# Where the second layer's low weight halves are computed on the GpSimd engine of a fused mixer and two-layer attention kernel

## What is computed

```python
h = shift_token(x)                      # half of the channels from the token before
q, k, v = split(h @ wqkv[l])            # 128 x 1536
q, k = rotary_xpos(l2norm(q) * qs, l2norm(k) * ks)
x = x + local_attention(q, k, v) @ wo[l]     # 8 heads of 64, windows of 64
h = layernorm(shift_token(x))
a, g = split(h @ w1[l] + b1[l])         # 128 x 682
x = x + (a * gelu(g)) @ w2[l] + b2[l]
```

## Time and profile before

| | us |
|---|---|
| median of 3 runs | 471.41 (470.22 to 472.78) |
| the profiled execution, its own time | 471.67 |
| its span in the trace | 469.9 |
| PE busy | 359.3 |
| DVE busy | 329.7 |
| POOL busy | 298.2 |
| ACT busy | 285.0 |
| mean granted TensorE clock | 0.916 of full speed |

### The profile page before, as it was taken

The page is one execution under the profiler, slowest core; times in us unless marked ns, Lnnn a source line. Parts: engine busy times, 40 slices in busy tenths (PEclk is TensorE's granted clock), DMA queues, the critical chain, the costliest instruction groups (busy, mean ns, idle before and its releaser), DMA issues.

```text
span 469.9 us, 11254 instructions
## 1 busy us (share of the span) xinstructions
PE 359.3 (76%) x3832; PEld 295.0 (63%) x3832; DVE 329.7 (70%) x744; ACT 285.0 (61%) x852; POOL 298.2 (63%) x248
## 2 busy tenths in 40 slices
PE   2573057898788998899899989998949896768362
PEld 1352036777676877687778767876838775656342
DVE  6879864678668768867877796768767866743423
ACT  3453075777676777777867867767827773664020
POOL 2200348999999499949975994899477958520212
PEclk9996575999999999999999999999979999797857
DMA  8500230511431052115113320431015201200100
GB/s 274 174 0 0 53 110 19 125 30 30 108 79 31 1 146 61 28 29 152 30 30 105 79 58 1 130 79 31 12 38 130 55 1 28 64 12 1 23 22 22
DMA packets 42399, 28.21 MB, mean 60 GB/s; under 512 B 21700, under 2 KB 36598, under 8 KB 42358
## 3 DMA queue, kind: packets, MB, share of 16 engines
q1 hardware_dynamic: 42357, 27.68, 22.7%
HBM read 13.51 MB, written 3.15 MB: 35 GB/s over the span
## 4 chain that ended last, share of the span: by engine, by line
PE 38%; DVE 22%; POOL 17%; issue 10%; ACT 7%; DMA 3%; SPq 2%; DVEq 1%; POOLq 0%; ACTq 0%
POOL rn L483 6%; PE bank L717 5%; DVE h L1083 4%; PE bank L682 4%; PE bank L554 4%; DVE rot_sin L1059 4%; PE bank L550 4%; PE upper L666 3%; PE bank L551 3%; DVE rot_cos L1059 3%; POOL rot L519 3%; ACT probs L833 2%; POOL rot L504 2%; PE bank L610 2%; POOL rot L505 2%
## 5 line engine op out<-in xcount | busy, mean ns | idle before, releaser
L833 ACT ACTIVATE probs<-upper,neg_max 128x128 f32<-128x128 f32 x256 | 90.4, 369 | 62.6 <-DVE neg_max L1105 62.6
L483 POOL TENSOR_TENSOR rn<-floored,minus_half 128x16 f32<-128x16 f32 x32 | 93.8, 2930 | 2.7
L504 POOL TENSOR_TENSOR rot<-rot_cos,rot_sin 128x512 f32<-128x512 f32 x32 | 40.9, 1278 | 64.9 <-DVE rot_sin L1059 47.1
L1105 DVE TENSOR_REDUCE neg_max<-upper 128x4 f32<-128x512 f32 x64 | 43.1, 683 | 34.4 <-PE upper L666 34.4
L519 POOL TENSOR_TENSOR rot<-rot,rn 128x1024 f32<-128x1024 f32 x32 | 60.9, 1903 | 1.9
L550 PE MATMUL bank<-wqkv_hi,act_t_hi 128*128 128x512 f32 x96 | 44.2, 460 | 21.4 <-DVE o_tok L1117 13.3
L833 ACT ACTIVATION_READ_ACCUMULATOR probs<-upper,neg_max 128x1 f32 x256 | 52.9, 207 | 0.0
L1059 DVE TENSOR_TENSOR rot_cos<-bank,tab 128x512 f32<-128x512 f32 x64 | 43.6, 682 | 2.7 <-PE bank L554 2.2
L1059 DVE TENSOR_TENSOR rot_sin<-bank,tab 128x512 f32<-128x512 f32 x64 | 43.5, 680 | 0.0
L1066 DVE TENSOR_REDUCE ss<-sq 128x16 f32<-128x1024 f32 x32 | 38.8, 1212 | 5.2 <-ACT sq L854 5.1
L550 PEld LDWEIGHTS bank<-wqkv_hi,act_t_hi 128*128 128x128 f32 x96 | 19.0, 198 | 36.0 <-issue 23.3
(11 more groups left out here) (129 smaller groups left out, 883.1 us busy)
## 6 DMA issues: line engine op xcount, KB each, us to landing
v_mid<-v_tok SPq DMA_DIRECT2D x64, 128.0 KB, 2.3
tab_raw<-tables SPq DMA_DIRECT2D x8, 512.0 KB, 3.3
h_tok<-group_in SPq DMA_DIRECT2D x14, 128.0 KB, 3.4
x_res<-group_in SPq DMA_DIRECT2D x28, 64.0 KB, 1.8
wqkv_raw<-wqkv SPq DMA_DIRECT2D x2, 768.0 KB, 6.7
x_in<-x SPq DMA_DIRECT2D x4, 256.0 KB, 3.4
head_scale<-head_scales SPq DMA_DIRECT2D x8, 128.0 KB, 3.9
group_in<-normed SPq DMA_DIRECT2D x4, 256.0 KB
```

The lines of the kernel that those rows point to most:

```text
L483: pool.tensor_tensor(rn[:, 0:2 * HEADS], floored[:, 0:2 * HEADS], minus_half[:, :], ALU.pow).then_inc(rn_ready, 1)
L504: pool.tensor_tensor(rot[cur.par][:, :, 0:32], rot_cos[:, :, 0:32], rot_sin[:, :, 32:64], ALU.add).then_inc(rot_added, 1)
L833: last = act.activation(probs[:, h, :], s_bank[half][:, (h % 4) * P:(h % 4 + 1) * P], ACT.Exp, bias=neg_max[a.par][:, h:h + 1], accum_out= ...
```

## The change

The five pieces after the tiles 3 to 6 go. In their place stand four instructions: in layer 0's hardware loop (G = 1 and 2), in step j = 2, POOL makes half of `wqkv_lo[1]` (768 columns) and half of `w1_lo[1]` (341 columns), right after the scaling of tile 4G + 5. The columns' offset comes from the register G. PE's wait counts 4 instead of 5.

```diff
-            def low_part(n):
+            def low_half(G):
 
                 pool.wait_ge(w_high, 4)
-                lo, raw, hi, cols = low_pieces(1)[n]
-                pool.tensor_tensor(lo[:, cols], raw[:, cols], hi[:, cols].bitcast(F32), ALU.subtract).then_inc(w_split, 1)
-
+                for lo, raw, hi, n in ((wqkv_lo[1], wqkv_raw[1], wqkv_hi[1], 3 * INNER // 2), (w1_lo[1], w1_raw[1], w1_hi[1], HID)):
+                    cols = bass.ds(G * n - n, n)
+                    pool.tensor_tensor(lo[:, cols], raw[:, cols], hi[:, cols].bitcast(F32), ALU.subtract).then_inc(w_split, 1)
...
-                    if number and G == 0:
-                        low_part(j)
-                        if j == GT - 1:
-                            low_part(GT)
+                    if not number and layer == 0 and j == 2:
+                        low_half(G)
...
                 if number and G == GROUPS - 1:
                     pe.wait_ge(w_high, 2 * DEPTH)
-                    pe.wait_ge(w_split, PIECES)
+                    pe.wait_ge(w_split, 4)
```

## The result

The changed kernel takes 467.47 us (median of 15 runs, 466.49 to 469.18) against 471.41 us before (15 runs). The ratio is 0.992, with a 95% interval of 0.9904 to 0.9936: 3.9 us saved. The forecast was 467.3 us.

A forecast was written before the change was run, and what follows sets the result against it. POOL was taken to set the pace in group G = 0. 5.41 us removed less 1.32 of waits for DVE, with the added work free: 471.67 - 4.1 = 467.6, or 467.3 us against the median; range 465.6 to 469.6 us.

The forecast's parts named there:

- What bounds group G = 0: From 90 to 130 us POOL sets the pace, busy 38.67 of 40 us, with the pieces standing without idle time.
- the ceiling: Group G = 0: removing the five pieces gives at most 5.41 us, priced between starts, if POOL alone sets the pace.
- the walk: Tiles 4 to 9: additions need POOL free and DVE's product, which moves by the gain two tiles earlier; 4.09 us arrive.
- How much arrives: Of the 5.41 us removed in G = 0, 1.32 become POOL's waits for DVE; about 4.1 reach G = 1's feed-forward.
- first three steps: Additions of tiles 4, 5 and 6 in G = 0 start earlier by 0.90, 2.12 and 3.34 us.
- the earliest start of the additions behind DVE's product: POOL's additions can start 0.81 us behind the start of DVE's last rotary product, taken from the feed-forward steps.
- the rival that POOL alone sets the pace: In G = 0 all 5.4 us removed arrive, 466.0 us; chance 0.13.
- The work added: Feed-forward steps of G = 1 and 2: low halves of 1.73 and 0.88 us, 2.6 together, covered by POOL's idle time.
- the cover: POOL's idle 6.95 us before its next additions in the feed-forward step hides the low halves, 3.6 us spare at worst.
- Do the low halves hold DVE up?: Feed-forward gates stay 0.75 us, cost nothing; rival: gates held, 4.4 us lost in all, 471.7 us, chance 0.04.
- The gain stays to the end: After G = 0 each group repeats as before, keeping about 4.1 us; rival: a fixed wait takes it back, 471.4 us, 0.06.
- The pace of the other engines: Rival in G = 0: PE or ACT closes the loop near 9.2 us a step; 2.5 us gained, 468.9 us, chance 0.14.

The follow-up runs named there:

- Both partial moves: Against the kernel before, only the w1 pieces moved to the feed-forward steps: 470.9 us; only the wqkv pieces moved there: 466.99 us.
- the one with three pairs: The changed kernel with two extra pairs of low halves per feed-forward step, written to buffers nobody reads: 469.79 us, ratio 0.9965 to the kernel before.

## Why the prediction was right

- **What bounds group G = 0.** Right: POOL, and the pieces stood in its chain. The 5.41 us of the ceiling, taken between starts, fit: tiles 5 and 6, ahead of which POOL does not wait, gained 1.24 and 1.22 us over the tile before, and the walk said 1.22 for both.
- **How much arrives.** The walk said 4.09 us at tile 9 and the trace shows 3.84. Its first three steps are right within 0.02 us. The term that was mis-sized is the earliest start of the additions behind DVE's product for tiles 7 and 8: it was 0.81 us, from the feed-forward step, and measured 0.91 and 0.90 (126.16 - 125.25 and 135.27 - 134.37); at tile 4 it was 0.81. Why it is longer at those two stays open. For tile 8 the product itself moved by 3.16 us instead of 3.34, and 0.18 and 0.09 make up the 0.27 us. The timelines of PE and ACT, of the kernel before (first fence) and the changed one, show where the 0.18 us went:

```profile
127.81 0.58 ACT L858 COPY probs_t<-upper 128x512 f32<-128x512 f32 x1
129.22 0.60 PE L617 MATMUL upper<-const,o_tok 128*128 128x128 f32 x4
129.75 0.27 PE L682 MATMUL bank<-v_mid,probs_t 128*64 128x64 f32 x1
```

```profile
126.45 0.58 ACT L856 COPY probs_t<-upper 128x512 f32<-128x512 f32 x1
126.66 0.60 PE L615 MATMUL upper<-const,o_tok 128*128 128x128 f32 x4
127.37 0.27 PE L680 MATMUL bank<-v_mid,probs_t 128*64 128x64 f32 x1
```

Counted from tile 3, PE's transposes ahead of the mixing moved by the full 3.35 us, but the mixing starts 0.71 us behind the start of the last of them instead of 0.53, and the scores of tile 6 follow it. The mixing needs ACT's copy of the probabilities. That copy belongs to the step of tile 7 and moved by 2.15 us only: it had ended 1.36 us before the mixing, and now ends 0.34 us before it. So a second path, which moves with the tile before, has caught up with the one of the walk. This is read from the rows and was not tried.

Both partial moves bear the walk out, 0.60 against 0.75 and 3.35 against 3.34, and the first of them excludes the rival that POOL alone sets the pace (1.75).

- **The work added.** Between starts the long piece measures 156.02 - 154.24 = 1.78 us for 1.73 taken; the short one's own duration is 0.90 for 0.88. It lies in idle time that is 7 us deep; the kernel without any low halves there is not shorter, and the one with three pairs pays just what exceeds the cover.
- **Do the low halves hold DVE up?** The gates no, as forecast from one row. (The second gate of the earlier trace rows, at 157.16, was not quite in POOL's idle time, as the prediction has it: POOL's scaling ends near 157.35.) The row of the copy was read rightly too: it is exposed, and 0.28 us longer when it meets POOL.
- **The gain stays to the end.** Right: 3.84 us at tile 9, 3.70 at the last tile.
- **The pace of the other engines.** It came out at 53.65 / 6 = 8.94 us a tile from tile 3 to 9, below the 9.2 of that rival. The rival was not wrong in kind: PE, busy for 35.02 of the 40 us from 90 to 130 before, is busy for 37.66 of them now, and has the largest part of the chain there.

The number itself, 467.3 for 467.47 us, is closer than the argument deserves, and that part is luck: the trace's gain was 0.25 us smaller than summed, and the runs spread over 2.7 us.

## What to carry to other kernels

Work taken off the engine that sets the pace counts only up to the next engine's data, and in a software pipeline those move by what was gained some steps earlier: walk it tile by tile, with start times, and the loss comes out of the trace before (5.4 us removed, 4.1 forecast, 3.8 measured). Idle time has to be chosen by what the other engines do in it: 7 us beside operands from PSUM took the work for nothing, 27 us beside a scan, subtractions and a minimum on operands in the core's memory did not. And a row that is slow because of a neighbour is worth its excess only up to the engine right behind it; ask for that engine before naming the gain.

## What the runs showed of the hardware that I had not expected

- Whether POOL and DVE hold each other up depends on the instruction's form. Beside POOL's subtractions the scan took 2.18 us instead of 1.28, a pair of subtractions of 341 columns 1.66 instead of 0.92, and a minimum with a scalar on 512 columns 1.12 instead of 0.43; normalising four tiles took 3.22 us instead of 1.27. The gates kept 0.75 us, and the residual 0.69. `h_lo`, two operands in the core's memory, kept 0.69 us beside POOL's power on 16 columns: not every POOL instruction does it. That power takes 2.93 us all the same.
- It costs POOL too: five pieces took 7.4 us in the mixer, and 5.4 us in group G = 0.
- An address that comes from a register costs nothing that is seen: the halves of 341 columns take 0.90 us with it and 0.88 without, and those of 768 columns (1.78 us between starts) lie on the line through 341 and 512 columns (1.73) within 0.1 us.
